# Batch 3's projections ahead of batch 1's values, and a new order of DVE's and ACT's work around the feed forward's start

## Chip, cores and metric

One core of a Trainium2 chip. The metric is the device time of one execution in microseconds, as the median of the runs shown. Batch, tile and unit numbers count from 0.

## What is computed

The inputs are x (4 x 512 x 512), ctx (4 x 512 x 256), the projection weights Wq and Wk (128 x 256), W1 (2048 x 512) and W2 (512 x 2048), all float32. Cut to what matters:

```python
n = layernorm(x)
q = ctx @ Wq.T + bq;  k = ctx @ Wk.T + bk
P = softmax(q @ k.T)
x = x + n @ P.T                       # values: contraction over the 512 positions
v = bf16(layernorm(x))                # residual of the feed forward
h = bf16(layernorm(v) * ln_w + ln_b)
y = gelu(bf16(mxq(h) @ mxq(W1).T + b1))
z = bf16(mxq(bf16(y)) @ mxq(W2).T + b2)
out = x + bf16(v + z)
```

`mxq` quantizes to 8 bits with one power-of-two scale for each block of 32 along the contracted axis: the largest magnitude of the block, its exponent, multiply by the inverse, clip at 127, multiply by the scale.

## The kernel before

There is one program for each engine, an instruction list written out by hand, and the order of these lists is the schedule; semaphores alone connect them. An engine takes its list strictly in order: an instruction that waits holds all behind it.

**First half, four batches of 512 rows in 4 tiles of 128.** For a batch, PE transposes ctx (`context`), projects it (`queries_keys`, 8 matmuls) and computes one energy tile per row tile (`energies(b, t)`, into two alternating PSUM banks, so energy t waits for the exp of t - 2). ACT copies out the transposed ctx (`context`) and the projections with their bias (`query_key`). DVE takes the negative row maximum (`negmax`), ACT the exp with its sum (`exp`), DVE the reciprocal (`recip`, `recip_scaled`), and ACT and DVE split the probabilities and the normalized x into a high and a low float16 part (`p_high`, `x_high` on ACT; `p_low`, `x_low` on DVE). SP transposes these by DMA (`p_transpose`, `x_transpose`). PE's `values(b, t)`, 12 float16 matmuls and a float32 one with the identity that adds x, needs all four transposed probability tiles of its batch and writes one of two PSUM banks; ACT evicts it with the sum of its rows (`x_plus`), so `values(b, t)` waits for `x_plus(b, t - 2)`. The next batch's transposes write the same buffer of x, and so wait for the values of the batch before. Around batch b's values the "front" of batch b + 1 is prepared.

**x1, v and h.** After `x_plus`, POOL computes the mean (`mean_x1`), ACT the squares (`x1_square`), POOL the factors (`factors_x1`), ACT v (`v_out`) and v's sums (`v_sums`, two passes, line 569 and 572), POOL the second layer norm's factors (`factors_v`), and DVE the scaled rows (`times_w`, `plus_b`, lines 1089 and 1094). `tail_parts(b)` lists DVE's steps for a batch: parts 0 to 3 are `times_w` and `plus_b` of one tile, part 4 is the reduction, exponent, scale and inverse of h1's quantization, part 5 its multiplication by the inverse, clip and multiplication by the scale.

**Weights.** W1 and W2 come in four units each, loaded by ACT's queue (`load_w1`, `load_w2`, lines 535 and 539) and quantized by DVE between the steps above: `w_amax`, `w_power`, `w_scale`, `w_inverse`, `w_over`, `w_clip`, `w_mult`; then transposed by SP. `front(b, ...)` holds DVE's steps for the front of a batch, `back(b, ...)` those between two fronts. Line 892 is the reduction for every kind of quantization, lines 900, 906 and 911 are its three small steps.

**Second half, 16 tiles i = 2m + k.** PE does `product1(i + 3)` (line 841) and `product2(i)` (line 851) in turn; ACT evicts the first (`y_evict`, line 656), computes the gelu (line 663) and evicts the second (`z_out`). DVE quantizes h2 in a slot for each tile: `slot(m, k, tail)` clips the tile before, reduces tile (m, k) (line 892), takes its exponent, multiplies the tile before by its scale (line 1006), and then the scale, the inverse and the multiplication (line 996) with the steps of `tail` in the gaps. SP transposes h2 behind line 1006, and product 2 waits for this. POOL adds the residual and x (`add_residual`, `add_x`, lines 471 and 477), for tile i not before DVE's clip of tile i + 3; POOL's list reaches them after `factors_v(3)`. The first two products of the second half stand between the values of batch 3: values(3, 0), values(3, 1), product1(0), values(3, 2), product1(1), values(3, 3), product1(2).

## Time and profile before

| | |
|---|---|
| median of 3 runs | 279.48 us (278.9 to 280.51) |
| the profiled execution | 279.64 us, of which the span is 277.8 us |
| busy in the span | PE 229.4 us (83%), DVE 242.8 us (87%), ACT 176.2 us (63%), POOL 67.7 us (24%) |
| granted TensorE clock, mean | 0.941 of full speed |
| chain that ended last | DVE 52%, PE 24%, DMA 9%, SP's queue 6%, ACT 3% |

The busy shares are means over two halves with different limits. The page in 40 slices of 6.9 us:

```profile
PE   7899989702799782909999797899999689999993
DVE  3499999653889999999979999999999999877992
ACT  2368497518298666876977799845655554565510
PEclk9999999965699998987999799999999999999998
```

Each digit is the busy share of a slice in tenths; PEclk is the granted clock in tenths. PE has gaps in the first half (near 55 to 70, 104 and 120 us) and few in the second; DVE is full from 70 to 235 us and has gaps in front of it and behind it. The times below are in microseconds from the span's start. A row of a timeline that joins several instructions gives their number (x12). Durations overlap the next start by some 0.1 us, so that lengths of a sequence are taken from start to start.

### The profile page before, as it was taken

The page shows a single profiled execution, that of the slowest core. Times are in us where ns is not written, and L with a number is a line of the kernel's source. Part 1 is how long each engine was busy: PE and PEld are TensorE (multiplying, and loading weights), DVE is VectorE, ACT ScalarE, POOL GpSimd, SP SyncE. Part 2 cuts the span into 40 slices and gives each one's busy share as a digit, 9 for nine tenths or more (in the row PEclk, how much of TensorE's full clock was granted, in tenths as well). Part 3 has the DMA queues.
Part 4 walks back from the last instruction along what each step waited for, and adds up shares of the span by engine and source line. Part 5 has one row for each costly group of instructions (what it writes and reads, how often), then busy time and mean ns, then how long its engine had stood idle before and what let it go on. Part 6 is the DMA issues. An engine that isn't in the chain of part 4 may idle for free.

```text
span 277.8 us, 3276 instructions
## 1 busy us (share of the span) xinstructions
PE 229.4 (83%) x975; PEld 102.0 (37%) x984; DVE 242.8 (87%) x354; ACT 176.2 (63%) x303; POOL 67.7 (24%) x101
## 2 busy tenths in 40 slices
PE   7899989702799782909999797899999689999993
PEld 6456434300344231303443233344444334444431
DVE  3499999653889999999979999999999999877992
ACT  2368497518298666876977799845655554565510
POOL 2094300202002600052160200363123333333400
PEclk9999999965699998987999799999999999999998
DMA  5999999999989945879032314565541565565683
GB/s 150 372 400 210 274 176 279 97 221 159 180 252 278 250 77 109 231 125 172 8 67 47 68 29 94 96 134 132 132 77 55 132 133 132 132 132 113 145 181 127
DMA packets 103077, 42.92 MB, mean 154 GB/s; under 512 B 93844, under 2 KB 96152, under 8 KB 102552
## 3 DMA queue, kind: packets, MB, share of 16 engines
q1 hardware_dynamic: 100224, 36.45, 63.5%
q10 hardware_dynamic: 2360, 6.30, 8.1%
q0 software_dynamic: 480, 0.02, 0.4%
q8 instruction: 5, 0.08, 0.1%
q14 instruction: 8, 0.07, 0.1%
HBM read 15.48 MB, written 4.19 MB: 71 GB/s over the span
## 4 chain that ended last, share of the span: by engine, by line
DVE 52%; PE 24%; DMA 9%; SPq 6%; ACT 3%; issue 2%; POOL 2%; DVEq 0%; POOLq 0%; ACTq 0%
DVE amax L892 14%; PE ps L851 9%; PE ps L773 6%; PE ps L841 5%; SPq L246 4%; DVE pf L1006 4%; DVE wquant L996 4%; DVE w_int L935 3%; DMA xhl<-pf 3%; DMA xs<-in_x 3%; DVE vw L1089 3%; DVE phl L1077 3%; DVE xhl L1082 3%; DVE hq L1094 3%; DMA pT<-phl 3%; DVE nmax L1063 3%
## 5 line engine op out<-in xcount | busy, mean ns | idle before, releaser
L851 PE MATMUL ps<-w2T,xhl 128*128 128x512 bf16 x247 | 56.5, 379 | 7.0 <-DMA xhl<-pf 6.7
L841 PE MATMUL ps<-w1T,cxT 128*128 128x512 bf16 x256 | 59.7, 388 | 0.0
L656 ACT ACTIVATE wst<-ps 128x1024 bf16<-128x1024 f32 x32 | 31.9, 1017 | 24.3 <-PE ps L841 24.3
L892 DVE TENSOR_REDUCE amax<-phl 128x64 f32<-128x2048 bf16 x16 | 36.5, 2280 | 4.0 <-ACT phl L663 4.0
L851 PEld LDWEIGHTS ps<-w2T,xhl 128*128 128x128 bf16 x256 | 24.3, 98 | 37.8 <-DMA xhl<-pf 8.8
L773 PE MATMUL ps<-pT,xT 128*128 128x512 f16 x96 | 25.9, 426 | 13.6 <-DMA pT<-phl 13.6
L841 PEld LDWEIGHTS ps<-w1T,cxT 128*128 128x128 bf16 x256 | 24.2, 99 | 33.9 <-issue 8.5
L663 ACT ACTIVATE phl<-wst 128x2048 bf16<-128x2048 bf16 x16 | 30.6, 1909 | 1.7 <-DVE wquant L996 0.6
L773 PE MATMUL ps<-h1q,xT 128*128 128x512 f16 x96 | 23.4, 396 | 6.7 <-ACT xs L546 6.0
L471 POOL TENSOR_TENSOR wst<-wst,vs 128x512 bf16<-128x512 bf16 x12 | 15.4, 1284 | 53.2 <-DVE wquant L1001 53.2
L761 PE MATMUL ps<-qkT 128*128 128x512 f32 x32 | 17.6, 648 | 11.9 <-ACT pf L506 10.3
L892 DVE TENSOR_REDUCE amax<-wst 128x64 f32<-128x2048 f32 x8 | 18.2, 2281 | 9.9 <-DMA wst<-in_L_ffn_W 9.9
L506 ACT ACTIVATE pf<-ps,nmax 128x512 f32<-128x512 f32 x16 | 10.9, 680 | 22.5 <-DVE nmax L1063 22.5
L676 ACT ACTIVATE wst<-ps 128x512 bf16<-128x512 f32 x16 | 9.5, 596 | 19.9 <-PE ps L851 19.9
L773 PEld LDWEIGHTS ps<-pT,xT 128*128 128x128 f16 x96 | 10.1, 107 | 31.1 <-issue 23.4
L407 POOL TENSOR_SCALAR mean<-sums 128x4 f32<-128x4 f32 x4 | 1.6, 396 | 71.4 <-ACT xs L546 71.4
L996 DVE TENSOR_TENSOR wquant<-phl,mxi 128x2048 int16<-128x2048 bf16 x15 | 18.3, 1223 | 0.3
L1006 DVE TENSOR_TENSOR pf<-wquant,mxs 128x2048 bf16<-128x2048 int16 x15 | 18.2, 1216 | 0.0
L773 PEld LDWEIGHTS ps<-h1q,xT 128*128 128x128 f16 x96 | 9.6, 101 | 22.2 <-issue 13.5
L546 ACT ACTIVATE xs<-ps,mr 128x512 f32<-128x512 f32 x16 | 10.8, 676 | 10.0 <-PE ps L776 9.9
L776 PE MATMUL ps<-xs,ident_x 128*128 128x512 f32 x32 | 16.3, 592 | 0.0
L935 DVE TENSOR_TENSOR w_int<-wst,mxi 128x2048 int16<-128x2048 f32 x7 | 16.0, 2283 | 0.0
(90 smaller groups left out, 383.9 us busy)
## 6 DMA issues: line engine op xcount, KB each, us to landing
wst<-in_L_ffn_W ACTq DMA_DIRECT2D x6, 1024.0 KB, 6.5
xs<-in_x SPq DMA_DIRECT2D x4, 1024.0 KB, 8.6
out_x<-wst SPq DMA_DIRECT2D x16, 256.0 KB, 3.0
cx<-in_ctx SPq DMA_DIRECT2D x4, 512.0 KB, 7.0
wst<-in_L_ffn_W SPq DMA_DIRECT2D x2, 1024.0 KB, 11.9
xhl<-pf SPq DMA_TRANSPOSE x17, 4.3
xT<-xhl SPq DMA_TRANSPOSE x16, 4.7
lnw<-in_L_ffn_ln_w SPq DMA_DIRECT2D x1, 256.0 KB, 3.7
```

The costliest lines, as they stand in the source:

```text
L471: pool.tensor_tensor(ws[:, k, :], zs[:, k, :], vs[:, i, :], ALU.add).then_inc(zv_rdy, 1)
L656: act.activation(ys[:, k, 1024 * g:1024 * g + 1024], ps_y[:, 2 * g:2 * g + 2, :], ACT.Copy)\
L663: act.activation(gs[:, k, :], ys[:, k, :], ACT.Gelu_apprx_tanh).then_inc(g_rdy, 1)
L761: pe.matmul(ps_e[:, t % 2, :], qkT[:, 0, P * t:P * t + P], qkT[:, 1, :], start=True, stop=True).then_inc(e_ps, 1)
L773: pe.matmul(ps_pv[:, t % 2, :], xT[:, t, NT * a + n, :], pTs[b % 2][:, :, NT * c + n, :], start=(s == 0), stop=False)
L776: pe.matmul(ps_pv[:, t % 2, :], ident_x[:, :], xs[:, LT * b + t, :], start=False, stop=True).then_inc(pv_ps, 1)
L841: last = pe.matmul(ps_y[:, c, :], h1T[:, k, t, :], w1T[:, 4 * c:4 * c + 4, t, :], start=False, stop=(t == KT - 1))
L851: last = pe.matmul(ps_z[:, k, :], h2T[:, k, t, :], w2T[:, t, :], start=False, stop=(t == FT - 1))
L892: dve.tensor_reduce(amax[:, a, :], by_block, AX_X, ALU.max, apply_absolute_value=True)\
L935: dve.tensor_tensor(blocks(w_int[:, :]), blocks(wst[:, a, :]), inverse, ALU.mult)\
L996: dve.tensor_tensor(pairs(h2u[:, k, :]), pairs(gs[:, k, :]), per_block(mxi[:, k, :, :]), ALU.mult).then_inc(h2_step[k], 1)
L1006: dve.tensor_tensor(pairs(h2q[:, k, :]), pairs(h2u[:, k, :]), per_block(mxs[:, k, :, :]), ALU.mult).then_inc(h2_step[k], 1)
```

## The change

On PE, where a batch has projections to do for the batch after next (that is batch 1, in the loop's `batch(1, 2, 3)`), `queries_keys(3)` and batch 2's energies 2 and 3 move ahead of batch 1's values, and batch 3's energies 0 and 1 move in among them: `energies(3, 0)` stands behind `values(1, 2)`, `energies(3, 1)` behind `values(1, 3)`. On ACT the generic `batch` is written out as three lists: `context(3)` moves into batch 0, `query_key(3, 0)` and `(3, 1)` move forward, batch 0's v rows in batch 1's list come later, and in batch 2's list `x_plus(2, 0)` and `x_plus(2, 1)` with v rows stand ahead of exp(3, 2). ACT takes `y_out(1, 1)` (eviction and gelu of tile 3) ahead of batch 3's `v_out`. On POOL the factors of v go ahead of the next mean. On DVE `front(2, ...)` is written out as `front_2`, with `negmax(2, 3)` four steps earlier, ahead of `w_over(W2, 1)`; W2's last unit goes ahead of batch 1's h1; and batch 2's layer norm rows, two tiles of which stood in front of the first slot, are spread over slots 0 to 2, its h1 over slots 3 and 4. From tile 5's slot on the lists are as before.

```diff
--- before.py
+++ after.py
@@ -446,9 +446,9 @@
 
             def batch(b, x, v):
 
-                mean_x1(b)
                 if v is not None:
                     factors_v(v)
+                mean_x1(b)
                 if x == 2:
                     factors_x_summed(x)
                 elif x is not None:
@@ -599,55 +599,106 @@
                 for t in range(LT):
                     x_square(2, t)
 
-            def batch(b, front, qk, v):
-
-
-                for t in range(LT + 1):
-                    if t < NT and t > int(b == 0):
-                        exp(front, t)
-                        x_high(front, t)
-                    if t > int(b == 0):
-                        p_high(front, t - 1)
-                    if t > 1:
-                        x_plus(b, t - 2)
-                    if v is not None and t == 1:
-                        v_out(v, 0)
-                    if v is not None and t > 0:
-                        v_sums(v, t - 1)
-                    if v is not None and 0 < t < LT:
-                        v_out(v, t)
-                    if t == 2:
-                        load_w2(front)
-                    if b == 0 and t == 3:
-                        act.wait_ge(e_ps, 2 * NT)
-                        query_key(2, 0)
-                        query_key(2, 1)
-                    if b > 0 and qk is not None and t == 3:
-                        context(qk)
-                if front + 1 < B:
-                    load_w1(front + 1)
-                x_plus(b, LT - 1)
-                if b > 0 and qk is not None:
-                    query_key(qk, 0)
-                x1_square(b, 0)
-                if b > 0 and qk is not None:
-                    query_key(qk, 1)
-                x1_square(b, 1)
-                x1_square(b, 2)
-                if front + 1 < B:
-                    exp(front + 1, 0)
-                    x_high(front + 1, 0)
-                x1_square(b, 3)
+            def batch_0():
+
+                exp(1, 2)
+                x_high(1, 2)
+                p_high(1, 1)
+                x_plus(0, 0)
+                load_w2(1)
+                exp(1, 3)
+                x_high(1, 3)
+                p_high(1, 2)
+                x_plus(0, 1)
+                act.wait_ge(e_ps, 2 * NT)
+                query_key(2, 0)
+                query_key(2, 1)
+                p_high(1, 3)
+                x_plus(0, 2)
+                load_w1(2)
+                x_plus(0, 3)
+                x1_square(0, 0)
+                x1_square(0, 1)
+                context(3)
+                x1_square(0, 2)
+                exp(2, 0)
+                x_high(2, 0)
+                x1_square(0, 3)
+
+            def batch_1():
+
+                exp(2, 1)
+                x_high(2, 1)
+                p_high(2, 0)
+                v_out(0, 0)
+                v_sums(0, 0)
+                v_out(0, 1)
+                exp(2, 2)
+                x_high(2, 2)
+                p_high(2, 1)
+                exp(2, 3)
+                x_high(2, 3)
+                act.wait_ge(e_ps, 3 * NT)
+                query_key(3, 0)
+                p_high(2, 2)
+                load_w2(2)
+                x_plus(1, 0)
+                p_high(2, 3)
+                v_sums(0, 1)
+                v_out(0, 2)
+                x_plus(1, 1)
+                query_key(3, 1)
+                v_sums(0, 2)
+                v_out(0, 3)
+                x_plus(1, 2)
+                v_sums(0, 3)
+                load_w1(3)
+                x_plus(1, 3)
+                x1_square(1, 0)
+                x1_square(1, 1)
+                x1_square(1, 2)
+                exp(3, 0)
+                x1_square(1, 3)
+                x_high(3, 0)
+
+            def batch_2():
+
+                exp(3, 1)
+                x_high(3, 1)
+                p_high(3, 0)
+                v_out(1, 0)
+                v_sums(1, 0)
+                v_out(1, 1)
+                x_plus(2, 0)
+                v_sums(1, 1)
+                v_out(1, 2)
+                x_plus(2, 1)
+                v_sums(1, 2)
+                v_out(1, 3)
+                exp(3, 2)
+                x_high(3, 2)
+                p_high(3, 1)
+                v_sums(1, 3)
+                x_plus(2, 2)
+                load_w2(3)
+                exp(3, 3)
+                x_high(3, 3)
+                p_high(3, 2)
+                x_plus(2, 3)
+                x1_square(2, 0)
+                x1_square(2, 1)
+                p_high(3, 3)
+                x1_square(2, 2)
+                x1_square(2, 3)
 
             context(0)
             act.wait_ge(ld_bqk, 32)
             query_key(0, 0)
             query_key(0, 1)
             first_batch()
-            batch(0, 1, 2, None)
-            for b in range(1, B - 2):
-                batch(b, b + 1, b + 2, b - 1)
-            batch(B - 2, B - 1, None, B - 3)
+            batch_0()
+            batch_1()
+            batch_2()
 
             def y_evict(m, k):
                 i = 2 * m + k
@@ -697,6 +748,7 @@
             y_out(1, 0)
             x1_square(B - 1, 2)
             x1_square(B - 1, 3)
+            y_out(1, 1)
             for t in range(LT):
                 v_out(B - 1, t)
 
@@ -705,7 +757,7 @@
                     y_out(*tile(m, k, 3))
                 z_out(m, k)
 
-            step(0, 0)
+            z_out(0, 0)
             v_sums(B - 1, 0)
             v_sums(B - 1, 1)
             step(0, 1)
@@ -781,14 +833,15 @@
 
                 if qk is not None:
                     context(qk)
+                    queries_keys(qk)
+                    energies(front, 2)
+                    energies(front, 3)
                 for t in range(LT):
-                    if t < NT - 2:
+                    if qk is None and t < NT - 2:
                         energies(front, t + 2)
                     values(b, t)
-                if qk is not None:
-                    queries_keys(qk)
-                    energies(qk, 0)
-                    energies(qk, 1)
+                    if qk is not None and t > 1:
+                        energies(qk, t - 2)
 
             def first_batches():
 
@@ -1183,6 +1236,37 @@
                 if h1 is not None:
                     h1_mult(h1)
 
+            def front_2():
+
+                w_amax(W1, 2)
+                x_low(2, 0)
+                w_power(W1, 2)
+                w_scale(W1, 2)
+                w_inverse(W1, 2)
+                negmax(2, 2)
+                recip(2, 1)
+                recip_scaled(2, 1)
+                p_low(2, 0)
+                negmax(2, 3)
+                x_low(2, 1)
+                w_over(W2, 1)
+                recip(2, 2)
+                x_low(2, 2)
+                recip_scaled(2, 2)
+                recip(2, 3)
+                p_low(2, 1)
+                recip_scaled(2, 3)
+                w_clip(W2, 1)
+                w_mult(W2, 1)
+                p_low(2, 2)
+                x_low(2, 3)
+                dve.wait_ge(w_step[W2], W_STEPS * 2)
+                w_over(W1, 2)
+                p_low(2, 3)
+                w_clip(W1, 2)
+                x_stats(3)
+                w_mult(W1, 2)
+
             def back(b, w2, tail):
 
 
@@ -1228,7 +1312,7 @@
             back(0, 0, None)
             front(1, 1, 0, None, None)
             back(1, 1, None)
-            front(2, 2, 1, 3, None)
+            front_2()
             dve.wait_ge(ld_ln, 32)
             back(2, 2, 0)
             for b in range(3, B):
@@ -1259,24 +1343,24 @@
                     h2_over(m, k)
 
 
+            w_over(W2, B - 1)
+            w_clip(W2, B - 1)
+            w_mult(W2, B - 1)
             for part in tail_parts(B - 3)[LT:]:
                 for part_step in part:
                     part_step()
-            w_over(W2, B - 1)
-            w_clip(W2, B - 1)
-            w_mult(W2, B - 1)
             parts = tail_parts(B - 2)
-            for part_step in parts[0] + parts[1]:
-                part_step()
             dve.wait_ge(w1T_rdy, 16 * B)
-            slot(0, 0, parts[2], True)
+            slot(0, 0, parts[0], True)
             dve.wait_ge(w2T_rdy, 16 * B)
-            slot(0, 1, parts[3] + parts[4])
-            slot(1, 0, parts[5])
+            slot(0, 1, parts[1])
+            slot(1, 0, parts[2] + parts[3])
+            slot(1, 1, parts[4])
+            slot(2, 0, parts[5])
             parts = tail_parts(B - 1)
-            parts = [[], [], parts[0], parts[1] + parts[2], parts[3] + parts[4], parts[5]]
-            for i in range(3, 3 + len(parts)):
-                slot(i // 2, i % 2, parts[i - 3])
+            parts = [parts[0], parts[1] + parts[2], parts[3] + parts[4], parts[5]]
+            for i in range(5, 5 + len(parts)):
+                slot(i // 2, i % 2, parts[i - 5])
             slot(LT, 1, [])
             with dve.Fori(LT + 1, T // 2 - 1) as m:
                 slot(m, 0, [])
```

## Rows read from the trace of the kernel before

**Rows 1.** Page, part 5: ACT's exps, with their idle time before.
```profile
L506 ACT ACTIVATE pf<-ps,nmax 128x512 f32<-128x512 f32 x16 | 10.9, 680 | 22.5 <-DVE nmax L1063 22.5
```

**Rows 2.** Timeline, DVE, 77 to 93 us: start, duration, line, tiles, idle time before.
```profile
77.14 0.69 DVE L1063 TENSOR_REDUCE nmax<-ps 128x1 f32<-128x512 f32 x1 [1.49 <-PE ps L761]
...
85.37 0.75 DVE L1077 SCALAR_TENSOR_TENSOR phl<-pf,rinv,phl 128x512 f16<-128x512 f32 x1 [0.38 <-ACT phl L512]
...
90.41 2.28 DVE L892 TENSOR_REDUCE amax<-wst 128x64 f32<-128x2048 f32 x1
...
92.82 0.69 DVE L1063 TENSOR_REDUCE nmax<-ps 128x1 f32<-128x512 f32 x1
```

**Rows 3.** Timeline, PE, the values blocks, 70 to 131 us.
```profile
70.86 4.53 PE L773 MATMUL ps<-pT,xT 128*128 128x512 f16 x12 [6.36 <-DMA pT<-phl]
...
109.27 4.10 PE L773 MATMUL ps<-h1q,xT 128*128 128x512 f16 x12 [6.01 <-ACT xs L546]
...
124.91 4.80 PE L773 MATMUL ps<-pT,xT 128*128 128x512 f16 x12 [7.24 <-DMA pT<-phl]
...
130.41 2.75 PE L773 MATMUL ps<-pT,xT 128*128 128x512 f16 x12
```

**Rows 4.** Timeline, ACT: exp(3, 0), exp(3, 2) and the first gelu.
```profile
93.55 0.69 ACT L506 ACTIVATE pf<-ps,nmax 128x512 f32<-128x512 f32 x1 [0.54 <-DVE nmax L1063]
...
106.45 0.69 ACT L506 ACTIVATE pf<-ps,nmax 128x512 f32<-128x512 f32 x1 [4.28 <-DVE nmax L1063]
...
143.49 1.91 ACT L663 ACTIVATE phl<-wst 128x2048 bf16<-128x2048 bf16 x1
```

**Rows 5.** Timeline, DVE, from `p_low(3, 3)` to the first h2 reduction.
```profile
119.72 0.74 DVE L1077 SCALAR_TENSOR_TENSOR phl<-pf,rinv,phl 128x512 f16<-128x512 f32 x1
...
131.91 2.29 DVE L892 TENSOR_REDUCE amax<-hq 128x64 f32<-128x2048 bf16 x1
...
143.63 0.75 DVE L1089 SCALAR_TENSOR_TENSOR vw<-vs,mean,lnw 128x512 f32<-128x512 bf16 x1 [1.21 <-POOL rs L375]
...
146.54 2.28 DVE L892 TENSOR_REDUCE amax<-phl 128x64 f32<-128x2048 bf16 x1
```

**Rows 6.** Chain that ended last, 120 us: start, duration, what.
```profile
120.49 4.03 DMA pT<-phl
```

**Rows 7.** Timeline, PE, its last wait of about 1 us: product 8.
```profile
227.78 3.63 PE L851 MATMUL ps<-w2T,xhl 128*128 128x512 bf16 x16 [0.98 <-DMA xhl<-pf]
```

**Rows 8.** Line 539, the three loads of W2: times from issue to landing.
```profile
DMA to landing us min/median/max: 5.5/6.8/15.4
```

**Rows 9.** Timeline, POOL: the last step of batch 0's layer norm factors.
```profile
90.63 1.04 POOL L375 TENSOR_TENSOR rs<-rs,half 128x4 f32<-128x4 f32 x1
```

**Rows 10.** Timeline, DVE, reductions that open the slots, 152 to 201 us.
```profile
152.58 2.28 DVE L892 TENSOR_REDUCE amax<-phl 128x64 f32<-128x2048 bf16 x1
...
162.50 2.28 DVE L892 TENSOR_REDUCE amax<-phl 128x64 f32<-128x2048 bf16 x1
...
171.05 2.28 DVE L892 TENSOR_REDUCE amax<-phl 128x64 f32<-128x2048 bf16 x1
...
176.96 2.28 DVE L892 TENSOR_REDUCE amax<-phl 128x64 f32<-128x2048 bf16 x1
...
184.80 2.28 DVE L892 TENSOR_REDUCE amax<-phl 128x64 f32<-128x2048 bf16 x1
...
192.07 2.28 DVE L892 TENSOR_REDUCE amax<-phl 128x64 f32<-128x2048 bf16 x1
...
200.65 2.28 DVE L892 TENSOR_REDUCE amax<-phl 128x64 f32<-128x2048 bf16 x1
```

**Rows 11.** Timeline, POOL and DVE, about 180 us.
```profile
179.86 1.75 POOL L471 TENSOR_TENSOR wst<-wst,vs 128x512 bf16<-128x512 bf16 x1
...
180.51 1.18 DVE L906 TENSOR_SCALAR mxs<-pow 128x128 bf16<-128x128 f32 x1
```

**Rows 12.** Windows, 125 to 132 us: busy time by engine, PEclk is the granted clock.
```profile
125.00:132.00 7.00, 7.00 (x22) 2.68 (x22) 6.82 (x13) 4.25 (x8) 1.45 (x4) 0.71 1.16 173
```

## The prediction

> **What bounds the kernel now.** The page's busy shares come first: DVE is the busiest engine, and ACT's largest waits are for it (22.5 us in front of the exps) [rows 1]. Then DVE's timeline, asking of each stretch what is late. After its two waits for weight loads, which end before 70 us and which the change doesn't touch, DVE is idle three times up to 93 us: 1.49 us in front of the row maximum of batch 2's tile 3, which PE had not computed because it stood behind `values(1, 0)`; 0.38 us ahead of `p_low(2, 3)`; and about 0.2 us ahead of batch 3's first row maximum (its start at 92.82 against 90.41 + 2.2 for the reduction in front of it) [rows 2]. From there DVE runs through to 142.4 us.
>
> PE is the opposite: 6.01 us idle for ACT's `x_plus(2, 0)`, which stands on ACT behind an exp that waits for DVE's row maximum, and 7.24 us for the last transposed part of batch 3's probabilities [rows 3, 4]. What ends that second wait is DVE's `p_low(3, 3)` at 119.72 us and then 4.03 us of DMA [rows 5, 6]. So up to batch 3's values the end is set by DVE; PE's and ACT's earlier waits are slack. From 124.91 us PE's chain values(3, 0), values(3, 1), product1(0), values(3, 2) leads to ACT's first gelu, which starts at 143.49 us and ends, by its successor's start, at 145.3 [rows 3, 4]. DVE reaches the first h2 reduction at 146.54 us, 1.2 us after it, because it first waited 1.21 us for POOL and did two layer norm tiles [rows 5]. Behind this DVE has no idle time until 237 us; PE waits for its transposes, last at 227.78 us by 0.98 us [rows 7], and from there PE sets the end. So what counts is the start of DVE's slot for tile 5 (184.80 us): from it to the end the order of the work is the same in both kernels.
>
> **Part 1: batch 3's projections and batch 2's last two energies ahead of batch 1's values.** ACT's `context(3)` and PE's `queries_keys(3)` go into the stretch before 62 us in which both engines wait for DVE's row maximum of batch 2's first tile: free. Both of batch 2's last energies are done by about 66.5 us, ahead of `values(1, 0)`, which waits for a transpose until 70.86 us in either kernel [rows 3]. Their second one needs ACT's exp at about 64.3 us, so nothing new is waited for. DVE now takes `negmax(2, 3)` at 72.7 us without waiting: 1.49 us gone. For the rest I lay ACT's list out by its durations, 0.6 to 0.7 us an operation [rows 1] and 1.4 us for the two passes of a v sum. `p_low(2, 3)` now comes behind `w_over(W1, 2)`, at 83.4 us; ACT's `p_high(2, 3)` is done by 79.4 us, behind `p_high(2, 2)` (which needs DVE's factor of 77.2 us) and `x_plus(1, 0)`: 0.38 us gone. `energies(3, 0)` is done by 84 us instead of 92.7: 0.2 us gone. **Sum: DVE is 2.07 us early**: `w_amax(W2, 2)` begins at about 88.4 us instead of 90.41, `negmax(3, 0)` at about 90.7 instead of 92.82 [rows 2].
>
> What may be late next is the load of W2's unit 2, issued by ACT at 78 us as before. Three such loads landed in 5.5, 6.8 and 15.4 us [rows 8]. With the median it is there at 84.8 us; 15.4 us (the first of them, issued close behind a load of x, which this one is not) would cost DVE 4.9 us. Then the factors of batch 0's layer norm: `v_sums(0, 3)` ends on ACT at about 86.6 us. In POOL's old order batch 1's mean (88.2 us) comes first, and the factors are there at 91.67 us as in the row [rows 9]; in the new order they take 3.1 us from 86.7 us, 89.8 us, and DVE wants them at 91.4 us. So this swap covers the 2.07 us by 1.6 us and gives 0.3. It makes batch 1's mean 1.7 us later (90.1 us), which holds ACT's squares; exp(3, 0) is then at 92.3 us, still before its 93.55 [rows 4], and DVE wants its sum at 95 us.
>
> **Part 2: batch 2's order on ACT.** `x_plus(2, 0)` and `x_plus(2, 1)` no longer stand behind the exp that waits for DVE. PE's 6.01 us go; `values(2, 3)` ends at 109 us, over 8 us earlier. Its worth is nothing: PE's next work waits for `p_low(3, 3)`. The other side: exp(3, 2) is now behind those evictions and v rows, at 105.4 us instead of 106.45 [rows 4]; DVE needs its sum at 108.9 us, 2.8 us after its end. exp(3, 3) ends at 110 us, wanted at 114 us; `p_high(3, 3)` at 115.5 us, wanted at 117.6. So the 2.07 us stay whole: `p_low(3, 3)` at 117.65 us, landed at 122.45, `values(3, 0)` at 122.83 us, the first gelu done at 143.2 us.
>
> **Part 3: DVE around the feed forward's start.** W2's last unit and batch 1's h1 change places: 10.5 us together (131.91 to 142.42) [rows 5], now from 129.8 us to 140.3. The two layer norm tiles of batch 2 (2.91 us, 143.63 to 146.54) leave this place, and with them the 1.21 us for POOL. But now DVE waits for the gelu: **3.0 us of new idle time**, and its first reduction begins at 143.3 us. That is 3.2 us early with 2.9 us of work still to do.
>
> The slots, from one reduction's start to the next [rows 5, 10]: 6.04 for (0, 0), with one layer norm pair, as before. A plain slot is 5.91 (171.05 to 176.96), and 0.15 more where POOL's adds lie beside its reduction. With one pair 7.27, with two 8.58 (both with the 0.15). So (0, 1) with one pair 7.12; (1, 0) with two 8.43; (1, 1) with h1's reduction and scales 9.92 less a pair of 1.45, 8.47; (2, 0) with h1's last three steps 8.55, as from 162.50 to 171.05. Sum 38.61: tile 5's slot would start at 181.9 us.
>
> To this comes a collision. In the trace POOL's first two adds (from 179.86 us) run beside DVE's two small scale operations, of which the first takes 1.18 us instead of 0.2 and the second the same; this slot is 7.84 us (176.96 to 184.80) instead of 5.91, 1.93 more [rows 10, 11]. After the change POOL gets there when `factors_v(3)` is done, at about 177 to 178 us (ACT's last v sum ends at 174.6 us, as its evictions all come 2 to 3 us earlier). DVE is then in slot (2, 0), behind its reduction, at `h1_over` and `h1_clip`: again 1.93 us, with the bounds 0 (POOL waits for each of DVE's operations until the next reduction) and 2.3 (both adds whole, at their usual length). I take 1.93, the nearest row. Tile 5's slot then starts at 183.86 us instead of 184.80.
>
> **Total: 0.94 us early.** The profiled execution of 279.64 us becomes **278.7 us**; against the median of 279.48, which is 0.16 lower, that is 0.3% less. PE doesn't take it back: DVE gates it at 227.78 us, and the 0.98 us of its wait there stay [rows 7].
>
> On interleaving, rows and notes differ. A layer norm pair costs 1.45 us where it stands alone and 1.2 to 1.3 inside a slot, since it fills gaps of 0.1 us between dependent small operations [rows 5, 10]. The Trainium skill ("VectorE: DVE Perf Modes", The DRAIN you can't avoid) says that the next operation can't issue until the pipe is empty, and that a semaphore between two costs nothing extra. By that the moved tiles would cost their full 2.91 us, and the gain would be 0.3 us.
>
> On the collision, DVE's small operations end with POOL's adds, to 0.1 us [rows 11]. The Trainium skill ("SBUF — State Buffer", SBUF: two separate sides) says that whichever of the two engines starts first holds the shared port pair for the whole instruction, and the other blocks. The trace agrees; by this rule POOL's adds aren't free wherever such an operation of DVE is under way.
>
> **Rivals.** *A: the collision goes.* If POOL's adds fall into a reduction, or wait for one, slot (2, 0) costs 8.55 us, and the time is 278.7 - 1.9 = 276.8 us. For it: DVE's operations there are longer, so POOL may lose the race. Against it: in the trace POOL got its turn after one such operation. A chance of 0.20. *B: nothing is left.* `values(3, 0)` comes 13.8 us after PE's last work instead of 7.24. In the trace its 12 matmuls take 4.80 us against 2.75 for a later block, and the granted clock is 0.71 from 125 to 132 us, which is 1.2 GHz for about 4 us of it and 2.4 for the rest [rows 3, 12]. If this whole values block (5.64 us, where 3.45 is usual) runs at 1.2 GHz it takes 6.9 us, the gelu is 1.26 us later and the time is 280.0 us. One late transpose does the same. 0.15. *C: slower.* The longer pause leaves PE at 1.2 GHz through values(3, 1) as well: 1.26 + 3.45 us later, 283.4 us. It decides the sign once the gelu is more than 0.94 us late; against it stand three restarts after waits of 6 to 7 us, which cost only 1.35 to 2.05 us each [rows 3]. 0.07, and 0.08 more for a weight load that is later than DVE (over 280.9 us). *D: DVE gains more than I count*, by a quicker restart of PE (4.10 us for the 12 matmuls is seen, 0.7 less) or a transpose that lands sooner: 277.7 us. 0.12. The forecast itself: 0.38.
>
> **How the numbers follow.** 0.5% (1.4 us) is about what a measurement of this kernel can tell. Faster than 278.1 us: A, D and a sixth of the forecast's own spread of 0.7 us, 0.38. Slower than 280.9: C, the late load and a rest of B, 0.17. Between: 0.45. The range leaves out C and a deeper A: 276.3 to 280.9 us.
>
> **What would show it.** Right: no idle time at `negmax(2, 3)`; `negmax(3, 0)` near 90.7 us; `p_low(3, 3)` near 117.7; PE's idle time ahead of values(3, 0) in one piece of some 13.8 us; DVE 3 us idle for the first gelu, at 140 to 143 us; two of DVE's operations stretched by about 1 us each near 178 us. Wrong: DVE waiting for `wst` after 88 us or for POOL's factors at 91 us, no wait for the first gelu, or DVE's lead at tile 5's slot not found again in PE's last wait at 227 us.

## The result and the profile after

The changed kernel takes 284.87 us, median of four executions (282.70 to 292.17), against 279.19 us (278.35 to 280.51) for the kernel before: **a ratio of 1.0173, 95% interval 1.0097 to 1.0249: slower, by between 1.0 and 2.5%**. Ratios here and below leave out the executions that took over 1.5% more than the fastest of their kernel (here the one of 292.17 us), and so aren't the quotients of the medians. The profiled execution took 282.70 us with a span of 280.9 us; before it was 279.64 and 277.8. The helper functions moved down: DVE's row maximum is now line 1116, the weight reduction line 945, `p_low` line 1130 and PE's values lines 825 and 828. Lines below 600 kept their numbers.

The page's slices of busy time come first (one digit for 7.0 us), then the shares of its chain.

```profile
PE   6899999681993799009999799986999789999993
DVE  2699999565999997869959999999999999877992
PEclk9999999977899589856999799999899999999999
...
DVE 42%; PE 28%; DMA 10%; SPq 9%; ACT 4%; issue 3%; POOL 3%; ACTq 0%; DVEq 0%; POOLq 0%
```

DVE was without gaps from 93 to 142 us [rows 2, 5]. Now it shows a 7 in slice 16 (105 to 112 us), a 6 in slice 18 (119 to 126 us) and a 5 in slice 21 (140 to 147 us). PE is at 0 in slices 17 and 18. The granted clock is at 5 in slice 18 and in slice 14 (91 to 98 us). Next, DVE's timeline (start, duration, line, tiles, idle time before), where the holes have names.

```profile
71.53 0.69 DVE L1116 TENSOR_REDUCE nmax<-ps 128x1 f32<-128x512 f32 x1
...
87.06 2.28 DVE L945 TENSOR_REDUCE amax<-wst 128x64 f32<-128x2048 f32 x1
...
89.25 0.68 DVE L1116 TENSOR_REDUCE nmax<-ps 128x1 f32<-128x512 f32 x1
...
109.24 0.16 DVE L1121 RECIPROCAL rinv<-rsum 128x1 f32<-128x1 f32 x1 [1.78 <-ACT pf L506]
...
121.68 0.75 DVE L1130 SCALAR_TENSOR_TENSOR phl<-pf,rinv,phl 128x512 f16<-128x512 f32 x1 [3.58 <-ACT phl L512]
...
147.38 2.29 DVE L945 TENSOR_REDUCE amax<-phl 128x64 f32<-128x2048 bf16 x1 [3.13 <-ACT phl L714]
...
187.79 2.28 DVE L945 TENSOR_REDUCE amax<-phl 128x64 f32<-128x2048 bf16 x1
```

The first three lines are part 1 as forecast. `negmax(2, 3)` has no idle time ahead of it (1.49 us before [rows 2]), nor does `negmax(3, 0)`. The next two are the loss: 1.78 us for the sum of exp(3, 2) and 3.58 us for `p_high(3, 3)`, neither of which DVE waited for before. Then comes the wait for the first gelu, 3.13 us. Tile 5's slot starts at 187.79 us against 184.80 [rows 10].

**Measured from a common point.** Absolute times mislead here. Both executions wait for weight loads, and DVE's fifth weight reduction, `w_amax(W1, 2)`, which opens this stretch, began at 67.74 us before and 66.56 us after. Over the executions profiled below it began anywhere from 57.3 to 72.5 us. I call this start S and give all times from S. (Whole executions of one kernel differ by more than 12 us for that reason, so the readings below rest on stretches and not on medians.)

| from S, us | before | after |
|---|---|---|
| `w_amax(W2, 2)` starts | 22.67 | 20.50 |
| `p_low(3, 3)` | 51.98 | 55.12 |
| slot of tile 0 (first gelu there) | 78.80 | 80.82 |
| slot of tile 5 | 117.06 | 121.23 |
| end of the span | 210.06 | 214.34 |

So a lead of 2.17 us becomes a lag of 3.14 us by `p_low(3, 3)`. That is a turn of 5.31 us, and the two waits sum to 5.36. Part 3 takes the lag to 2.02 us and then to 4.17 us, and from there it reaches the end: 4.28 us. The two spans differ by 3.1 us only, since S was 1.18 us earlier in the second.

**Where exp(3, 2) lost its time.** ACT's timeline: the evictions `x_plus(2, 0)` and `x_plus(2, 1)`, exp(3, 2), batch 2's first square, and `p_high(3, 3)`.

```profile
101.44 0.69 ACT L546 ACTIVATE xs<-ps,mr 128x512 f32<-128x512 f32 x1 [2.84 <-PE ps L828]
...
105.69 0.69 ACT L546 ACTIVATE xs<-ps,mr 128x512 f32<-128x512 f32 x1 [1.40 <-PE ps L828]
...
108.45 0.67 ACT L506 ACTIVATE pf<-ps,nmax 128x512 f32<-128x512 f32 x1
...
119.52 0.72 ACT L554 ACTIVATE vs<-xs,mean 128x512 bf16<-128x512 f32 x1 [4.49 <-POOL mean L407]
...
120.94 0.70 ACT L512 ACTIVATE phl<-pf,rinv 128x512 f16<-128x512 f32 x1
```

Both evictions wait for PE, 2.84 and 1.40 us, and exp(3, 2) stands behind them and their v rows. PE's timeline, the block values(2, 0), values(3, 0) and product 8; then values(2, 0) in the kernel before.

```profile
95.34 5.15 PE L825 MATMUL ps<-h1q,xT 128*128 128x512 f16 x12 [1.41 <-DMA h1q<-phl]
...
126.83 4.78 PE L825 MATMUL ps<-pT,xT 128*128 128x512 f16 x12 [14.28 <-DMA pT<-phl]
...
230.81 3.63 PE L904 MATMUL ps<-w2T,xhl 128*128 128x512 bf16 x16 [1.01 <-DMA xhl<-pf]
```

```profile
95.34 2.75 PE L773 MATMUL ps<-h1q,xT 128*128 128x512 f16 x12
```

The 12 matmuls of values(2, 0) take 5.15 us instead of 2.75. Windows (us, busy time of PE, PEld, DVE, ACT and POOL, granted clock, DMA share, GB/s), after and then before:

```profile
95.00:101.00 6.00, 5.66 (x14) 2.30 (x15) 5.90 (x9) 3.54 (x8) 0.00 (x0) 0.56 1.05 193
...
118.00:125.00 7.00, 0.00 (x0) 0.00 (x0) 3.31 (x5) 3.54 (x9) 3.18 (x5) 0.50 0.39 74
```

```profile
95.00:101.00 6.00, 6.00 (x25) 2.59 (x24) 5.93 (x12) 4.32 (x10) 2.11 (x3) 1.00 0.92 168
```

From 95 to 101 us the clock was 0.56 of full speed after (1.2 GHz for nearly all of it) and full speed, 2.4 GHz, before. PE had been idle for 4.83 and 1.41 us just before. In the kernel before, batch 3's projections filled that gap, and it is part 1 that moved them away. What PE waited for is a transposed part, which SP issues. SP's DMA list and ACT's weight loads, by issue:

```profile
77.13 6.02 SPq L246 DMA_TRANSPOSE h1q<-phl  x1
...
85.97 4.07 SPq L239 DMA_TRANSPOSE xT<-xhl  x1
```

```profile
75.91 0.34 ACTq L539 DMA_DIRECT2D wst<-in_L_ffn_W  x1
...
84.60 0.39 ACTq L535 DMA_DIRECT2D wst<-in_L_ffn_W  x1
```

A transpose that is usually issued in 1.23 us takes 6.02 us when it follows a load of 1 MB by 1.2 us, and 4.07 us behind the next. (That the loads are the cause is read from this order in time; no run moves them. In the kernel before, the first of the two took 3.08 us.) SP issues the last two parts of batch 2's probabilities from 90.08 us on, and `values(2, 0)` starts at S + 28.78 us.

**Where `p_high(3, 3)` lost its time.** It stands behind two squares, and the squares wait 4.49 us for the mean. POOL's timeline, with two steps left out (1.22 and 0.65 us): `factors_v(1)`, which stood behind the mean in the kernel before and now stands ahead of it, and the mean. Then two of DVE's operations at that time, `x_low(3, 3)` and `w_over`.

```profile
111.96 1.25 POOL L421 TENSOR_SCALAR mean<-sums 128x4 f32<-128x4 f32 x1 [17.46 <-ACT vs L572]
...
115.37 2.79 POOL L429 TENSOR_TENSOR rs<-ms,mean 128x4 f32<-128x4 f32 x1
...
118.23 1.04 POOL L375 TENSOR_TENSOR rs<-rs,half 128x4 f32<-128x4 f32 x1
...
119.25 0.23 POOL L407 TENSOR_SCALAR mean<-sums 128x4 f32<-128x4 f32 x1
```

```profile
115.15 0.74 DVE L1135 SCALAR_TENSOR_TENSOR xhl<-xs,rs,xhl 128x512 f16<-128x512 f32 x1
...
115.81 2.28 DVE L988 TENSOR_TENSOR w_int<-wst,mxi 128x2048 int16<-128x2048 f32 x1
```

`x_plus(2, 3)` was finished at 115.0 us, and the mean itself takes 0.23 us, yet it starts at 119.25 us. The five operations of `factors_v(1)` took 7.3 us. The first four, on four elements a partition, take 0.20 to 0.29 us each at 139.6 us, where DVE is in a reduction or in its small operations; the fifth takes 1.04 us in either place. Here the one at 115.37 us lies beside both of DVE's operations shown and ends 0.07 us after `w_over` does.

**The slots.** DVE's reduction that opens slot (2, 0), and the two stretched scale operations in it:

```profile
177.34 2.28 DVE L945 TENSOR_REDUCE amax<-phl 128x64 f32<-128x2048 bf16 x1
...
182.04 1.17 DVE L959 TENSOR_SCALAR mxs<-pow 128x128 bf16<-128x128 f32 x1
...
183.73 1.14 DVE L964 TENSOR_SCALAR mxi<-mxs 128x128 uint16<-128x128 uint16 x1
```

The slots from tile 0 to tile 5 last 6.08, 7.11, 8.43, 8.34 and 10.45 us. The prediction had 6.04, 7.12, 8.43, 8.47 and 10.48.

### The profile page after: what moved, and what is told of

It reads as the page before. It is cut to its first block, busy times and chain, and to the rows that moved or that the text cites. A ratio compares the mean times of both kernels' runs of the same rounds, so it can differ in the third digit from the quotient of the medians.

```text
span 280.9 us, 3278 instructions
## 1 busy us (share of the span) xinstructions
PE 232.6 (83%) x975; PEld 102.5 (36%) x984; DVE 242.0 (86%) x354; ACT 175.8 (63%) x303; POOL 70.4 (25%) x101
## 4 chain that ended last, share of the span: by engine, by line
DVE 42%; PE 28%; DMA 10%; SPq 9%; ACT 4%; issue 3%; POOL 3%; ACTq 0%; DVEq 0%; POOLq 0%
DVE amax L945 12%; PE ps L825 10%; PE ps L904 9%; PE ps L894 6%; SPq L246 5%; DVE pf L1059 4%; DVE wquant L1049 4%; SPq L239 3%; DMA xhl<-pf 3%; DMA xs<-in_x 3%; DMA pT<-phl 3%; PE ps L828 2%; DVE wquant L1054 2%; DVE phl L1130 2%; DVE hq L1147 2%
## 5 line engine op out<-in xcount | busy, mean ns | idle before, releaser
L904 PE MATMUL ps<-w2T,xhl 128*128 128x512 bf16 x247 | 58.0, 387 | 7.0 <-DMA xhl<-pf 6.6
L825 PE MATMUL ps<-pT,xT 128*128 128x512 f16 x96 | 25.6, 423 | 20.4 <-DMA pT<-phl 20.4
L825 PE MATMUL ps<-h1q,xT 128*128 128x512 f16 x96 | 24.4, 409 | 2.0 <-DMA h1q<-phl 2.0
L805 PE MATMUL ps<-cxT,wqkT 128*128 128x512 f32 x32 | 16.3, 658 | 2.7 <-ACT cxT L496 2.7
```

The costliest lines, as they stand in the source:

```text
L805: last = pe.matmul(ps_qk[:, a, :], wqkT[:, a, c, :], cxT[:, c, :], start=(c == 0), stop=(c == CT - 1))
L825: pe.matmul(ps_pv[:, t % 2, :], xT[:, t, NT * a + n, :], pTs[b % 2][:, :, NT * c + n, :], start=(s == 0), stop=False)
L904: last = pe.matmul(ps_z[:, k, :], h2T[:, k, t, :], w2T[:, t, :], start=False, stop=(t == FT - 1))
```

## The experiments

The stretches, in us from S, with DVE's waits between S and tile 0's slot:

| kernel | `w_amax(W2, 2)` | `p_low(3, 3)` | tile 0 | tile 5 | end of span | waits of DVE |
|---|---|---|---|---|---|---|
| before | 22.67 | 51.98 | 78.80 | 117.06 | 210.06 | 1.49, 0.38, 1.21 |
| before, again | 23.87 | 53.17 | 79.99 | 118.25 | 211.28 | 2.69, 0.38, 1.21 |
| after | 20.50 | 55.12 | 80.82 | 121.23 | 214.34 | 1.78 exp, 3.58 p_high, 3.13 gelu |
| after, again | 20.57 | 56.80 | 82.01 | 122.41 | 216.01 | 3.38 exp, 3.58 p_high, 2.63 gelu |
| after, POOL's old order | 22.46 | 60.70 | 86.79 | 127.12 | 220.16 | 2.46 loads, 1.99 PE, 6.30 exp, 3.53 gelu |
| the same again | 20.50 | 52.14 | 77.99 | 118.32 | 211.91 | 2.48 exp, 3.29 gelu |
| after, `p_high(3, 3)` ahead of the squares | 20.50 | 50.97 | 76.56 | 116.98 | 210.56 | 1.28 exp, 3.02 gelu |
| after, exp(3, 2) early | 20.50 | 51.46 | 77.91 | 118.22 | 211.30 | 0.62, 1.06, 3.88 gelu |
| after, both | 20.49 | 51.18 | 77.39 | 117.72 | 210.82 | 0.35, 1.06, 3.65 gelu |
| after, ACT's old batch 2 | 20.50 | 49.58 | 76.57 | 117.03 | 210.13 | 4.39 gelu |
| part 1 alone | 20.50 | 49.59 | 76.40 | 114.67 | 208.26 | 1.21 |
| part 1 alone, again | 20.50 | 49.92 | 76.75 | 115.00 | 208.04 | 0.24, 1.21 |
| part 2 alone | 23.89 | 55.95 | 83.10 | 121.36 | 214.45 | 2.70, 0.38, 0.53, 2.28 p_high, 1.55 |
| part 3 alone | 23.81 | 53.12 | 78.70 | 119.11 | 212.12 | 2.62, 0.38, 2.98 gelu |

The two profiles of the kernel before differ by 1.2 us, all of it in PE's lateness at `negmax(2, 3)`, which hangs on a transpose. So 1 us between two rows is within the spread, unless the wait that makes it is named.

### Both kernels again

The changed kernel and the kernel before, without an edit, to see which waits recur.

> The changed kernel once more, timed on the same chip as the three below. Theory S (POOL's factors of v, stretched beside DVE, hold back the mean of batch 2, behind which stand ACT's squares and behind these p_high(3, 3)) and rival T (the cost lies in the second half, in the new slots and in PE's wait of 2.74 us for product 4) both expect 282.5 to 285 us, with 3 to 4 us of DVE idle time ahead of p_low(3, 3) and POOL needing over 6 us for factors_v(1).

> The kernel before once more, for a second trace of it: how much its stretches from w_amax(W1, 2) move by themselves. All theories: 51.5 to 53.5 us to p_low(3, 3), no DVE wait for exp(3, 2) or p_high(3, 3) in front of it, slots of 38.3 us from tile 0 to tile 5, 116.6 to 118.5 us to tile 5's slot, whatever the time of the whole.

Medians of six executions, and of eleven for the kernel before beside them: 281.39 us for the changed kernel where the kernel before had 278.61; and 279.92 for the kernel before again where it had 277.3. The second number is a comparison of a kernel with itself, so 2.6 us between medians of this size says nothing. The stretches do: the mean from S to the end is 215.2 us after and 210.7 before, **4.5 us or 1.6%**, which agrees with the ratio of 1.0173. DVE's timeline of the changed kernel again:

```profile
115.06 0.16 DVE L1121 RECIPROCAL rinv<-rsum 128x1 f32<-128x1 f32 x1 [3.38 <-ACT pf L506]
...
127.49 0.75 DVE L1130 SCALAR_TENSOR_TENSOR phl<-pf,rinv,phl 128x512 f16<-128x512 f32 x1 [3.58 <-ACT phl L512]
```

The wait for `p_high(3, 3)` is the same to 0.01 us. The one for exp(3, 2) is twice as long, and values(2, 0) started at S + 31.5 us, 2.7 us later than in the first profile. Both waits belong to the change; the size of the exp's differs with the end of values(2, 0), as is worked out below.

### POOL's order

```diff
 def batch(b, x, v):          # POOL
+    mean_x1(b)
     if v is not None:
         factors_v(v)
-    mean_x1(b)
```

> POOL's order alone put back: the mean of x1 ahead of the factors of v, in every batch. Theory S: the mean of batch 2 is there within 1.5 us of x_plus(2, 3), p_high(3, 3) ends before 118 us, the 3.6 us of DVE idle time ahead of p_low(3, 3) fall to 0 to 1, and the time is 2.5 to 3.6 us below the changed kernel's. The 1.8 us of DVE idle time for exp(3, 2) stay. DVE may wait up to 0.5 us for batch 0's factors near 90 us. Rival T: no more than 0.5 us below the changed kernel, as the slots still start behind the gelu.

> The changed kernel with POOL's old order, again, since values(2, 0) of the first look waited 9.2 us for its transposes and hid the rest. Theory S: mean_x1(2) within 1.5 us of x_plus(2, 3), no DVE wait ahead of p_low(3, 3), the wait for exp(3, 2) there in full (1.8 us with values(2, 0) 29 us behind w_amax(W1, 2), and one more for each us that these are later). Rival (the wait ahead of p_low(3, 3) has another cause than POOL's order): 3.6 us of it again.

Medians of six: 282.32 us (278.61 before) and 281.78 us (277.3 before, ratio 1.0376, 1.0246 to 1.0506). In the first profile the loads and transposes came late: DVE waited 2.46 us for weights. PE and DVE, with idle time before:

```profile
108.53 5.28 PE L825 MATMUL ps<-h1q,xT 128*128 128x512 f16 x12 [9.21 <-DMA h1q<-phl]
...
122.96 0.16 DVE L1121 RECIPROCAL rinv<-rsum 128x1 f32<-128x1 f32 x1 [6.30 <-ACT pf L506]
```

values(2, 0) waited 9.21 us for its transpose (SP's issues beside loads took 8.38 and 6.61 us there) and started at S + 37.5 us; DVE then waited 6.30 us for exp(3, 2). There was no wait at `p_low(3, 3)` in it, but with everything so late that didn't decide; hence the repetition. POOL, ACT and DVE of the second:

```profile
121.73 0.23 POOL L407 TENSOR_SCALAR mean<-sums 128x4 f32<-128x4 f32 x1 [20.59 <-ACT xs L546]
...
121.92 2.87 POOL L421 TENSOR_SCALAR mean<-sums 128x4 f32<-128x4 f32 x1
...
123.42 0.71 ACT L512 ACTIVATE phl<-pf,rinv 128x512 f16<-128x512 f32 x1
...
124.63 0.74 DVE L1130 SCALAR_TENSOR_TENSOR phl<-pf,rinv,phl 128x512 f16<-128x512 f32 x1
```

The mean now runs as soon as `x_plus(2, 3)` is done, and the stretched operation (2.87 us) comes behind it, where nobody waits. `p_high(3, 3)` is done in time, and DVE's `p_low(3, 3)` shows no idle time. It starts at S + 52.14 us instead of 55.12 and 56.80. **So POOL's new order makes the 3.58 us wait.** The exp's wait, 2.48 us, is left.

### `p_high(3, 3)` ahead of the squares

```diff
 x_plus(2, 3)                 # ACT, batch_2
+p_high(3, 3)
 x1_square(2, 0)
 x1_square(2, 1)
-p_high(3, 3)
```

> ACT's p_high(3, 3) ahead of x1_square(2, 0) and (2, 1) instead of behind them; POOL's order stays the new one. Theory S: POOL's factors_v(1) still takes over 6 us and the squares still wait for it, but DVE no longer does: the same 2.5 to 3.6 us below the changed kernel as with POOL's old order. If the stretched POOL chain cost anything by another way (v_out of batch 2 comes 4 us later), this kernel stays slower than a1 by that. Rival T: within 0.5 us of the changed kernel.

Median 279.31 us, 278.61 before (ratio 1.0192, 1.0037 to 1.0348). POOL has its new order here: `factors_v(1)` takes 8.3 us in all (114.55 to 122.84), longer than in the changed kernel. DVE doesn't wait for it: `p_low(3, 3)` is at S + 50.97 us. Here the late POOL is harmless: nothing that DVE wants soon stands behind it on ACT.

### exp(3, 2) early, and both edits

```diff
 v_out(1, 2)                  # ACT, batch_2
+exp(3, 2)
+x_high(3, 2)
+p_high(3, 1)
 x_plus(2, 1)
 v_sums(1, 2)
 v_out(1, 3)
-exp(3, 2)
-x_high(3, 2)
-p_high(3, 1)
```

> Only exp(3, 2) ahead of x_plus(2, 1); p_high(3, 3) stays behind the squares. Theory S: DVE's wait for exp(3, 2) (1.8 us, 3.4 in the second look) goes, but the wait ahead of p_low(3, 3) stays at 3.6 or grows by what the other one gives back, as it hangs on POOL: 119 to 121.2 us from w_amax(W1, 2) to tile 5's slot. If the two waits are independent it is 119.4, if the second swallows the first 121.2.

> The changed kernel with p_high(3, 3) ahead of batch 2's squares and exp(3, 2) ahead of x_plus(2, 1) on ACT, which takes away what either of DVE's two new waits waits for. As a whole execution moves by several us with its weight loads, I measure from the start of w_amax(W1, 2) to p_low(3, 3) and to the slot of tile 5: 52.0 and 117.1 us before, 55.1 and 121.2 in the changed kernel. Theory S (both waits are the whole loss, and the slots cost 2.15 us more than before): 49.6 to 50.2 and 115.3 to 116.2 us; median 0.5 to 2 us below the kernel before. Rival T (the second half's new slots lose on their own): 117 us or more to tile 5's slot, since the gelu doesn't come earlier.

Both: 282.85 us median; exp alone: 276.08; the kernel before beside them 276.07. The exp's wait is gone in either (0.62 and 0.35 us are left for exp(3, 3), and 1.06 us for `p_high(3, 2)`), and this although values(2, 0) was later, S + 30.2 and 30.4 us. That supports the coupling through `x_plus(2, 1)`. But with the exp alone, where `p_high(3, 3)` kept its place, I had expected its wait to stay, and it went too. POOL (the first step of `factors_v(1)`) and ACT (`p_high(3, 3)`):

```profile
105.24 0.67 POOL L421 TENSOR_SCALAR mean<-sums 128x4 f32<-128x4 f32 x1 [17.50 <-ACT vs L572]
...
110.07 0.71 ACT L512 ACTIVATE phl<-pf,rinv 128x512 f16<-128x512 f32 x1
```

Here `factors_v(1)` fell for the most part into DVE's own idle time (its waits of 0.62 and 1.06 us, at 105.8 to 107.7 us). It took 2.7 us (105.24 to 107.92) instead of 7.3, and the mean was there as soon as `x_plus(2, 3)` was. **The stretch is no fixed cost of POOL's order**; it was there when DVE's `w_clip`, `w_mult`, `x_low(3, 3)` and `w_over` lay beside it.

### ACT's batch 2 as before

```diff
 v_out(1, 1)                  # ACT, batch_2
+exp(3, 2)
+x_high(3, 2)
+p_high(3, 1)
 x_plus(2, 0)
...
-exp(3, 2)
-x_high(3, 2)
-p_high(3, 1)
...
+p_high(3, 3)
+x_plus(2, 2)
...
 x1_square(2, 1)
-p_high(3, 3)
```

> Batch 2's list on ACT in the order of the kernel before (exp(3, 2) ahead of x_plus(2, 0), p_high(3, 3) ahead of x_plus(2, 2)); all else as changed. Theory S: both of DVE's new waits go, 1.8 and 3.6 us; DVE's lead of 2 us over the kernel before reaches p_low(3, 3), PE idles about 6 us for x_plus(2, 0) again, and the time is that of my forecast: 0.3 to 1.5 us below the kernel before, 4 to 5.4 below the changed one. Rival T: 2 us or more above the kernel before, as the second half is unchanged.

Median 277.94 us, 278.61 before (ratio 1.0112, 0.9977 to 1.0246). DVE waits for nothing up to `p_low(3, 3)`, at S + 49.58 us: the lead of part 1 is whole, 2.4 us ahead of the kernel before. Yet tile 0's slot is no earlier than with `p_high(3, 3)` moved alone. ACT and PE, from batch 2's first square on:

```profile
122.52 0.72 ACT L554 ACTIVATE vs<-xs,mean 128x512 bf16<-128x512 f32 x1 [4.90 <-POOL mean L407]
...
128.40 2.93 ACT L561 ACTIVATE vs<-xs,off,rs 128x512 bf16<-128x512 f32 x4 [2.95 <-POOL off L415]
...
131.24 0.67 ACT L546 ACTIVATE xs<-ps,mr 128x512 f32<-128x512 f32 x1
...
140.09 0.40 PE L889 MATMUL ps<-b1row,ones 3*128 3x512 bf16 x4 [1.88 <-ACT wst L707]
```

ACT waits 4.90 us for the mean, which again stands behind `factors_v(1)` (5.2 us here), and then 2.95 us for POOL's `off` of batch 2, with `x_plus(3, 0)` queued behind v's four rows. PE had finished that tile's product at 127.3 us; it is evicted at 131.24. PE's bias step then waits 1.88 us for ACT. From `p_low(3, 3)` to tile 0's slot it takes 27.0 us, where it takes 25.7 in the changed kernel and 25.6 with `p_high(3, 3)` moved (25.2 to 26.5 in the others with this tail and the new list).

These 1.3 us look like the worth of part 2's order on ACT, which I had put at nothing. The runs of the next section don't bear that out. With part 1 alone, that is with the same lead and the same old list on ACT but POOL's old order too, v's rows begin 7.1 us behind `p_low(3, 3)` (at 115.66 against 108.53 us) instead of 11.5, and the first gelu begins 23.3 and 23.7 us behind it in two profiles, instead of 25.0:

```profile
115.66 2.93 ACT L561 ACTIVATE vs<-xs,off,rs 128x512 bf16<-128x512 f32 x4 [2.73 <-POOL off L415]
```

With part 3 alone, again with both old orders, the gelu begins after 23.6 us and the slot after 25.6. So the 1.3 us are a second cost of POOL's new order, which the new list on ACT hides. (Parts 1 and 3 together with both old orders weren't run.)

### The parts alone

Part 1 alone: the kernel before with PE's order, ACT's lists of batches 0 and 1 and DVE's `front_2`; ACT's batch 2, POOL's order and the tail as before.

```diff
+def batch_0(): ...           # ACT, as in the change
+def batch_1(): ...
+def batch_2():               # the order of before
...
-front(2, 2, 1, 3, None)      # DVE
+front_2()
```

> The kernel before with part 1 alone: PE's order, ACT's batches 0 and 1, DVE's front_2; batch 2 on ACT, POOL's order and the second half as before. Theory S: DVE's lead of 2.07 us reaches p_low(3, 3) (49.6 to 50.0 us from w_amax(W1, 2)) and, since the start of the second half hangs on it, tile 5's slot: 115.0 us, 1.5 to 2.1 us faster than the kernel before. If POOL's old order makes DVE wait for batch 0's factors, up to 0.5 us of it is lost. Rival T agrees on p_low and sees the same 115.

> The kernel before with part 1 alone, again, for its time: it was 2.4 us shorter to p_low(3, 3) and to tile 5's slot than the kernel before, and 1.8 to the end. Theory S: the same again within 0.5 us: 49.6 and 114.7 us; as a median 1 to 2 us below the kernel before if the spread of the loads lets it be seen.

Medians 275.99 us (276.07 before) and 276.80 us (277.3 before). Tile 5's slot is at S + 114.67 and 115.00 us against 117.06 and 118.25, and the end at 208.26 and 208.04 against 210.06 and 211.28. `p_low(3, 3)` is at 49.59 and 49.92. In the second, DVE waited 0.24 us for batch 0's factors, which come late in POOL's old order; the prediction gave that swap 0.3 us.

Part 2 alone: the kernel before with the new list for ACT's batch 2 and POOL's new order.

```diff
+    if v is not None:        # POOL
+        factors_v(v)
     mean_x1(b)
...
-batch(B - 2, B - 1, None, B - 3)
+batch_2()                    # ACT, the new order
```

> The kernel before with part 2 alone: batch 2's new list on ACT and POOL's new order; PE, DVE and the second half as before. Theory S (the new list makes DVE wait for exp(3, 2) as soon as values(2, 1) end later than DVE's row maximum): DVE is 2 us later here than in the changed kernel, so the wait is 0 to 1.5 us where the changed kernel had 1.8 and 3.4; with values(2, 0) more than 30 us behind w_amax(W1, 2) it is over 1. The wait ahead of p_low(3, 3) is 3 to 4 us if POOL's factors_v(1) falls on h1_clip, w_clip, w_mult and w_over(W1, 3), else 0. So 52 to 57 us to p_low(3, 3), never less than before. A gain would refute S.

Median 281.44 us, 277.3 before (ratio 1.0235, 1.0170 to 1.0299). DVE's wait for `p_high(3, 3)` is there, 2.28 us (`factors_v(1)` takes 6.7 us and the mean behind it 2.1), and there is none for exp(3, 2): DVE isn't early here, and PE, which still has batch 3's projections in this place, runs values(2, 0) in 2.75 us. Tile 5's slot is at S + 121.36 us, 3.1 us behind the kernel before again, whose first wait (2.69 us) is the same.

Part 3 alone: the kernel before with the tail's order and ACT's `y_out(1, 1)` and `z_out(0, 0)`.

```diff
+w_over(W2, B - 1)            # DVE
+w_clip(W2, B - 1)
+w_mult(W2, B - 1)
 for part in tail_parts(B - 3)[LT:]: ...
-w_over(W2, B - 1)
...
-slot(0, 0, parts[2], True)
+slot(0, 0, parts[0], True)
...
-slot(0, 1, parts[3] + parts[4])
-slot(1, 0, parts[5])
+slot(0, 1, parts[1])
+slot(1, 0, parts[2] + parts[3])
+slot(1, 1, parts[4])
+slot(2, 0, parts[5])
```

> The kernel before with part 3 of the change alone (W2's last unit ahead of h1, layer norm rows of batch 2 in the slots, ACT's y_out(1, 1) ahead of v_out). Theory S: first reduction right behind the gelu, 1.1 us earlier than before, then slots that are 2.1 us longer: 118.1 us from w_amax(W1, 2) to tile 5's slot (117.1 before) and 0.5 to 1.5 us slower. Rival T (part 3 is where the change loses): 120 us or more. A gain here would speak against both.

Median 282.34 us, 276.07 before (ratio 1.0144, 0.9932 to 1.0356). DVE's first h2 reduction:

```profile
149.78 2.29 DVE L893 TENSOR_REDUCE amax<-phl 128x64 f32<-128x2048 bf16 x1 [2.98 <-ACT phl L663]
```

The gelu's wait is 2.98 us without any lead from part 1. Against the kernel before again, with the same first wait, tile 0's slot is 1.29 us early and tile 5's 0.86 us late. The slots take 40.41 us in this kernel too.

## Why the prediction was wrong

Taken one at a time, to tile 5's slot, the parts come to -2.4 and -3.3 us (part 1, first and second profiles), +3.1 (part 2) and +0.9 (part 3), some 1.1 us in sum. Together they come to +4.2: the exp's wait arises only where parts 1 and 2 meet, and the wait for `p_high(3, 3)` is larger there, 3.58 us against 2.28.

1. **Part 1: right.** DVE's lead was put at 2.07 us and is 2.17; all three waits went. The load of W2's unit and POOL's swap were rightly found to be no obstacle (in one later profile DVE did wait 1.88 us for that unit, the late load of the last rival).
2. **Part 2, exp(3, 2): the step that failed first.** The prediction had it at 105.4 us on the scale of before, S + 37.7, "2.8 us after its end" before DVE wants its sum. It was at S + 41.9, 4.2 us later. These are ACT's two waits for PE in front of it, 2.84 and 1.40 us, which the layout of ACT's list had at nothing. Of the 4.2 us the block at 1.2 GHz makes 2.4 (5.15 us instead of 2.75); the other 1.8 go to the start of values(2, 0), behind a stopped list of SP. I had named this restart only for values(3, 0), and hadn't asked what PE does in the gap from which part 1 takes its work. 4.2 less the slack of 2.8 is 1.4; DVE waited 1.78 us, since it was itself 0.3 us earlier than drawn.

   How long DVE waits can be told from one number, the end of the twelve matmuls of values(2, 0). After (95.34 us above), then with `p_high(3, 3)` moved, POOL's old order again, and the changed kernel again:

```profile
98.44 4.65 PE L825 MATMUL ps<-h1q,xT 128*128 128x512 f16 x12 [0.85 <-DMA h1q<-phl]
...
101.88 5.23 PE L825 MATMUL ps<-h1q,xT 128*128 128x512 f16 x12 [3.08 <-DMA h1q<-phl]
...
102.19 4.12 PE L825 MATMUL ps<-h1q,xT 128*128 128x512 f16 x12 [4.13 <-DMA h1q<-phl]
```

   The ends lie at S + 33.93, 33.45, 34.62 and 35.62 us and the waits are 1.78, 1.28, 2.48 and 3.38 us: each is the end less 32.2, to 0.1 us. So at full clock the first three starts (S + 28.78, 28.80 and 29.39) would have cost next to no wait, by this estimate, and only the fourth (S + 31.50) is late enough to cost one, of 2.1 us. The term missing from the prediction's sum is the slow block of values(2, 0).
3. **Part 2, `p_high(3, 3)`: the larger failure.** It was put at 115.5 us, S + 47.8, and came at S + 54.4, 6.6 us late. Of this 4.5 us are ACT's wait for `mean_x1(2)`, moved behind `factors_v(1)`, while two squares stand ahead of `p_high(3, 3)`; the other 2.1 us came with the delay just named. The prediction priced POOL's swap for batch 1, where it gains, and not for batch 2, where the same line makes a mean wait for five operations whose length depends on DVE. It had cited a stretched DVE operation beside POOL [rows 11] without turning the row round: POOL's small operations are stretched as well.
4. **Part 2's worth "nothing": right.** With ACT's old list and POOL's old order, part 1's lead reached `p_low(3, 3)` and the first gelu whole, in two profiles. The old list cost 1.3 us only under POOL's new order.
5. **Part 3: right in its size.** The prediction had it cost 1.13 us (2.07 less 0.94); alone it cost 0.9. The gelu's wait was put at 3.0 us and is 3.13; the slots at 40.54 and are 40.41. In the collision the size was right and the place was not: POOL reached its adds at 181.85 us instead of 177 to 178, and they struck the two scale operations (1.17 and 1.14 us), as in the kernel before, and not the steps of h1. PE's last wait is 1.01 us, put at 0.98, so the change in tile 5's slot reached the end whole.
6. **Interleaving.** The moved layer norm tiles, 2.91 us in one place, made the slots 2.15 us longer (40.41 less 38.26). So a quarter was saved, as the rows had it. The Trainium skill ("VectorE: DVE Perf Modes", The DRAIN you can't avoid) would by my reading have given no saving; the trace doesn't bear that reading out here, and the section itself says that an operation that is not held starts earlier.
7. **Rivals.** A, no collision: slots of 40.3 to 40.5 us in all nine profiles with this tail speak against it. B and C, a slow restart of values(3, 0): after 14.28 us of idle time, about as long as forecast, its 12 matmuls take 4.78 us against 4.80 after 7.24 us [rows 3]. A pause twice as long costs nothing more, though the granted clock was 0.50 from 118 to 125 us. D, a quicker restart: not in the first profile, but in the second (4.23 us), where the gelu's wait was 0.5 us shorter. The slower case did come, but not by the mechanism that I gave it, nor by the late weight load. One reading of rows was off: the whole block of values(3, 0) is 5.50 us from start to start [rows 3], not 5.64, so that B would have been 0.14 us slower.

What stays open: what sets the start of values(2, 0) (S + 28.8 to 31.5 us in the four profiles above, 37.5 in the one with late loads, where DVE was itself some 4 us late and still waited 6.30 us). It hangs on SP's transposes, but a kernel in which `load_w2` or `load_w1` is issued later wasn't run, nor one that keeps PE busy ahead of the block.

**The best version** is the kernel before with part 1 alone. From S to the end it takes 208.15 us (mean of two) against 210.67, **2.5 us or 0.9% less**. By medians it can't be told from the kernel before.

## What to carry to other kernels

When an engine's list is rearranged, a slack counts only if each thing newly put ahead is priced at its worst row: here a slack of 2.8 us was drawn against transposes and a helper engine whose durations vary from 1.2 to 6 us and from 0.2 to 2.8 us in one trace. Work that the critical engine wants goes ahead of evictions and means that hang on DMA or on GpSimd; moving `p_high(3, 3)` up by two places took away a wait of 3.58 us. When work is moved out of a gap, ask what the engine's clock does in the gap it leaves, and compare kernels from a common point inside the trace when the time of the whole is moved more by its loads than by the change.
